# Two long attentions: the first maximum's scores through three rotating bank pairs, with the value projections between them

## The reference: a four-layer perceiver, of which two cross-attentions matter

```python
def _L1_xattn_ref(x, context, Wq, bq, Wk, bk, Wv, bv, Wo, bo):
    q = x @ Wq.T + bq                       # (1, 64, 128), 16 heads of 8
    k = context @ Wk.T + bk                 # (1, 6272, 128)
    v = context @ Wv.T + bv
    ...
    attn = jnp.einsum('bihd,bjhd->bhij', q, k) * SCALE
    attn = jax.nn.softmax(attn, axis=-1)
    out = jnp.einsum('bhij,bjhd->bihd', attn, v)
    out = out.reshape(B, NQ, IN_DIM)
    return out @ Wo.T + bo

x = x + _L1_xattn_ref(_layernorm(x, axis=-1), ctx_768, L1_xattn_Wq, ...)
```

## Time and profile before

| | us |
|---|---|
| median of 3 executions | 663.24 (662.68 to 671.8) |
| the profiled execution | 663.12 |
| its span in the trace | 661.3 |
| level 1: first to last PE instruction of the first maximum | 161.6 to 177.7 |
| level 3: the same | 527.5 to 543.8 |

### The profile page before, as it was taken

The page is one execution under the profiler, slowest core; times in us unless marked ns, Lnnn a source line. Parts: engine busy times, 40 slices in busy tenths (PEclk is TensorE's granted clock), DMA queues, the critical chain, the costliest instruction groups (busy, mean ns, idle before and its releaser), DMA issues. The chain is left out here.

```text
span 661.3 us, 11985 instructions
## 1 busy us (share of the span) xinstructions
PE 513.6 (78%) x4815; PEld 324.5 (49%) x4815; DVE 434.1 (66%) x828; ACT 299.6 (45%) x367; POOL 132.1 (20%) x197
## 2 busy tenths in 40 slices
PE   8799996788889997438995594782578488999857
PEld 5456673575355564313442263472456335556546
DVE  6744325856967955744999999925556596785243
ACT  2578881425557685111654560020112164768611
POOL 2111000000000000204688999400100000000000
PEclk9989997989899999556998587795569679999959
DMA  8364481563200000001022035052300150000000
GB/s 218 72 185 117 128 321 57 173 181 80 94 2 2 1 3 1 3 0 50 0 84 111 0 147 124 5 116 55 127 1 1 31 256 1 2 2 2 2 0 3
DMA packets 17674, 45.59 MB, mean 69 GB/s; under 512 B 4281, under 2 KB 13674, under 8 KB 16778
## 3 DMA queue, kind: packets, MB, share of 16 engines
q1 hardware_dynamic: 17556, 44.72, 22.3%
q0 software_dynamic: 64, 0.11, 0.1%
HBM read 34.28 MB, written 8.29 MB: 64 GB/s over the span
## 5 line engine op out<-in xcount | busy, mean ns | idle before, releaser
L251 POOL TENSOR_TENSOR rstd<-rstd,minus_half 64x1 f32<-64x1 f32 x20 | 11.8, 589 | 420.3 <-DVE rstd L259 420.3
L1497 ACT ACTIVATE ring<-psum,l3x_gain_columns 128x1024 f32<-128x1024 f32 x49 | 54.4, 1114 | 23.2 <-PE psum L1389 23.2
L1497 ACT ACTIVATE ring<-psum,l1x_gain_columns 128x1024 f32<-128x1024 f32 x49 | 54.4, 1114 | 22.4 <-PE psum L1389 22.4
L1403 PE MATMUL psum<-ring,values 128*32 128x128 f32 x1568 | 62.7, 279 | 0.4 <-ACT ring L1497 0.4
L934 ACT ACTIVATE ring<-psum,l0x_key_scale 128x1024 f32<-128x1024 f32 x49 | 52.1, 1114 | 8.2 <-PE psum L827 8.2
L1403 PEld LDWEIGHTS psum<-ring,values 128*32 128x32 f32 x1568 | 37.0, 109 | 28.1 <-issue 24.7
L1602 DVE TENSOR_REDUCE l1x_tops<-psum 128x1 f32<-128x448 f32 x64 | 36.7, 619 | 10.2 <-PE psum L1378 10.1
L1602 DVE TENSOR_REDUCE l3x_tops<-psum 128x1 f32<-128x448 f32 x64 | 36.7, 619 | 10.2 <-PE psum L1378 10.1
L3186 DVE MAX8 l2x_best<-values 128x8 f32<-128x6272 f32 x6 | 40.1, 6691 | 0.1
L3194 DVE MATCH_REPLACE8 values<-l2x_best,values 128x6272 f32<-128x6272 f32 x6 | 40.1, 6675 | 0.0
L827 PE MATMUL psum<-l0x_Q_stack,wide 96*128 96x256 f16 x196 | 29.8, 281 | 4.2 <-ACT ring L934 2.1
(11 more groups left out here) (778 smaller groups left out, 1080.7 us busy)
## 6 DMA issues: line engine op xcount, KB each, us to landing
wide<-keys_aside SPq DMA_DIRECT2D x54, 224.0 KB, 3.8
experts<-in_experts SPq DMA_DIRECT2D x1, 4608.0 KB, 13.5
experts<-in_experts SPq DMA_DIRECT2D x1, 4096.0 KB, 15.3
keys_aside<-ring SPq DMA_DIRECT2D x7, 448.0 KB, 2.5
keys_aside<-experts SPq DMA_DIRECT2D x6, 448.0 KB, 3.2
ring<-in_ctx_tiles SPq DMA_DIRECT2D x1, 2352.0 KB, 9.3
experts<-in_experts SPq DMA_DIRECT2D x1, 2048.0 KB, 7.8
ctx_t<-in_ctx_t SPq DMA_DIRECT2D x3, 672.0 KB, 7.4
```

Source lines behind the costliest of these rows:

```text
L1403: last = nc.tensor.matmul(ps[32 * quarter:32 * quarter + 32, O_BANK, 128 * half:128 * half + 128], mem.values[:, at:at + 32], probs[:, t % ...
L1497: nc.scalar.activation(probs[:, t % PROBS, :].rearrange("p (b n) -> p b n", b=2), ps[:, pair:pair + 2, :], ACT.Exp, scale=exp_gain[:, :]). ...
```

## The change: bank pairs in turn, values in between, queries' stack in halves

The 24 pairs of the first maximum now take the banks (0,1), (2,3), (4,5) in turn, and each pair waits for the reader of the pair three places before it. The values' projections no longer stand ahead of all scores: they use banks 6 and 7, and super `late_values[n]` is projected behind the last pair of round n. It waits until the super before it is copied, and ACT copies super n - 1 behind its two copies of round n. `Q_stack` is announced in two halves of two groups each (`Q_stack0`, `Q_stack1`). DVE copies the stack before the last low parts of the keys, not behind them, and copies the later chunks' stacks and computes the residual behind `raise_top(0)`. Of the two copies that end `raise_top(0)` the second goes to ACT (`first_top`).

```diff
@@ PE
-                    if n >= ready + 2:
-                        pe.wait_ge(values_copied, n - ready - 1)
+                    if n > ready:
+                        pe.wait_ge(values_copied, n - ready)
...
-                        last = nc.tensor.matmul(ps[:, 4 + 2 * (n % 2) + j // 4, (j % 4) * C:(j % 4 + 1) * C],
+                        last = nc.tensor.matmul(ps[:, VALUE_BANKS[j // 4], (j % 4) * C:(j % 4 + 1) * C],
...
-                for n in late_values:
-                    project("V", n)
-                pe.wait_ge(*act_done.at("Q_stack"))
-                pe.wait_ge(*dve_done.at("Q_stack"))
                 if late_keys:
                     pe.wait_ge(low_ready, len(late_keys))
-                pe.wait_ge(values_copied, len(late_values))
-
-                for n, s in first:
+                for n, s, p in pairs:
...
                     pe.wait_ge(*stacked_with(u))
-                    for g in range(G):
-                        if n >= 1 and g % 2 == 0:
-                            pe.wait_ge(*first_read(n - 1, s, g // 2))
-                        last = nc.tensor.matmul(ps[:, s * G + g, 0:HALF], ...
+                    pe.wait_ge(*act_done.at(f"Q_stack{p}"))
+                    pe.wait_ge(*dve_done.at(f"Q_stack{p}"))
+                    if at >= 3:
+                        pe.wait_ge(*first_read(*pairs[at - 3]))
+                    for g in (2 * p, 2 * p + 1):
+                        last = nc.tensor.matmul(ps[:, pair_bank(n, s, p) + g % 2, 0:HALF], ...
+                    last.then_inc(first_scores, 1)
+                    if (s, p) == (1, 1) and n < len(late_values):
+                        project("V", late_values[n])
@@ ACT
-                for n in late_values[0:2]:
-                    copy_values(n)
                 act.wait_ge(*dve_done.at("Q_parts"))
                 for g in range(G):
                     ins = nc.scalar.activation(Q_stack[64:96, 0, g, :], Q_low[32 * g:32 * g + 32, :], ACT.Identity)
-                ins.then_inc(*act_done.mark("Q_stack"))
-                for n in late_values[2:]:
-                    copy_values(n)
+                    if g % 2 == 1:
+                        ins.then_inc(*act_done.mark(f"Q_stack{g // 2}"))
                 for n, s in copied:
...
+                    if 1 <= n <= len(late_values):
+                        copy_values(late_values[n - 1])
+                act.wait_ge(top_turned, 2)
+                nc.scalar.activation(Q_stack[96:98, 0, :, :].rearrange("p g n -> p (g n)")[:, 512:1024],
+                                     ps[96:98, SLOTS[1], :], ACT.Identity).then_inc(*act_done.mark("first_top"))
@@ DVE
-                for n in late_keys[2:]:
-                    low(n)
                 for g in range(G):
                     for block_row in range(2):
                         ins = v.tensor_copy(Q_stack[32 * block_row:32 * block_row + 32, 0, g, :], ...
-                ins.then_inc(*dve_done.mark("Q_stack"))
...
+                    if g % 2 == 1:
+                        ins.then_inc(*dve_done.mark(f"Q_stack{g // 2}"))
+                for n in late_keys[2:]:
+                    low(n)
```

More of the change, by code:

```diff
@@ L1195, in stage_long_attention @@
     late_values = list(range(ready, SUPERS))
-    act_done.stage("Q_stack", *["factors"][:N_CHUNKS - 1])
+    act_done.stage("Q_stack0", "Q_stack1", "first_top", *["factors"][:N_CHUNKS - 1])
     pe_done.stage("xnT", "QT", "own", "projected")
-    dve_done.stage("var", "xn", "xnT", "Q_parts", "Q_stack",
+    dve_done.stage("var", "xn", "xnT", "Q_parts", "Q_stack0", "Q_stack1",
                    *["below", "factor_rows"][:2 * (N_CHUNKS - 1)], "weighed", "OT", "x")
@@ L1217, in stage_long_attention, with queries_with @@
         sem("scores_ready"), sem("probs_ready"), sem("pv_done"), sem("o_saved"))
+    def queries_with(k):
+        return q_ready, 2 * k + 1
     def stacked_with(u):
@@ L1223, in stacked_with, with pair_bank @@
         return stacked, 16 * PER_STACK
+    pairs = [(n, s, p) for n, s in first for p in range(2)]
+    def pair_bank(n, s, p):
+        return 2 * (pairs.index((n, s, p)) % 3)
     def first_read(n, s, p):
@@ L1333, in _ @@
                     project("K", n)
-                for n in late_values:
-                    project("V", n)
-                pe.wait_ge(*act_done.at("Q_stack"))
-                pe.wait_ge(*dve_done.at("Q_stack"))
                 if late_keys:
                     pe.wait_ge(low_ready, len(late_keys))
-                pe.wait_ge(values_copied, len(late_values))
-                for n, s in first:
-                    u, half = n // 2, slice((n % 2) * HALF, (n % 2 + 1) * HALF)
+                for n, s, p in pairs:
+                    u, half, at = n // 2, slice((n % 2) * HALF, (n % 2 + 1) * HALF), pairs.index((n, s, p))
                     pe.wait_ge(*stacked_with(u))
-                    for g in range(G):
-                        if n >= 1 and g % 2 == 0:
-                            pe.wait_ge(*first_read(n - 1, s, g // 2))
-                        last = nc.tensor.matmul(ps[:, s * G + g, 0:HALF], Q_stack[0:96, 0, g, 128 * s:128 * s + 128],
+                    pe.wait_ge(*act_done.at(f"Q_stack{p}"))
[3 more added lines that the diff above has]
+                    for g in (2 * p, 2 * p + 1):
+                        last = nc.tensor.matmul(ps[:, pair_bank(n, s, p) + g % 2, 0:HALF],
+                                                Q_stack[0:96, 0, g, 128 * s:128 * s + 128],
                                                 stack[0:96, u, g, half], start=True, stop=True)
-                        if g % 2 == 1:
-                            last.then_inc(first_scores, 1)
+                    last.then_inc(first_scores, 1)
+                    if (s, p) == (1, 1) and n < len(late_values):
+                        project("V", late_values[n])
                 def turn_top(k):
@@ L1356, in turn_top @@
                     for b in range(2):
-                        bank = slot((q_ready, 2 * k + b + 1))
+                        read = act_done.at("first_top") if k == 0 and b == 1 else (q_ready, 2 * k + b + (k == 0))
+                        bank = slot(read)
                         for j in range(4):
@@ L1384, in scores @@
                     pe.wait_ge(*stacked_with(u))
-                    pe.wait_ge(q_ready, 2 * k + 2)
+                    pe.wait_ge(*queries_with(k))
+                    if t == 0:
+                        pe.wait_ge(*act_done.at("first_top"))
                     if t >= RING:
@@ L1413, in keep_on @@
                                          start=True, stop=True)
-                pe.wait_ge(*first_read(first[-1][0], 0, 0))
+                pe.wait_ge(*first_read(*[pair for pair in pairs if pair_bank(*pair) == 0][-1]))
                 keep_on(14)
@@ L1531, in _ @@
                 v.tensor_tensor(Q_low[:, :], whole, Q_high[:, :], ALU.subtract).then_inc(*dve_done.mark("Q_parts"))
-                for n in late_keys[2:]:
-                    low(n)
+                dve.wait_ge(*dve_done.at("Q_parts"))
                 for g in range(G):
@@ L1558, in raise_top @@
                     for b in range(2):
+                        bank = SLOTS[next(slots) % len(SLOTS)]
+                        if (k, b) == (0, 1):
+                            continue
                         dve.wait_ge(top_turned, 2 * k + b + 1)
-                        bank = SLOTS[next(slots) % len(SLOTS)]
                         v.tensor_copy(Q_stack[96:98, k, :, :].rearrange("p g n -> p (g n)")[:, 512 * b:512 * b + 512],
@@ L1594, in _ @@
                 raise_top(0)
+                dve.wait_ge(*act_done.at("Q_stack1"))
+                dve.wait_ge(*dve_done.at("Q_stack1"))
+                for k in range(1, N_CHUNKS):
+                    v.tensor_copy(Q_stack[0:96, k, :, :], Q_stack[0:96, 0, :, :])
+                step(v.tensor_tensor(residual[:, :], mem.x[:, :], mem.row(f"{pack}_bo"), ALU.add))
                 for k in range(1, N_CHUNKS):
```

18 lines of the change are left out of this document (10 added, 8 removed).

## The result

The changed kernel took 690.06 us (median of 4: 692.68, 690.4, 689.71, 682.83) against 664.88 us before (4: 662.68 to 671.8). The ratio of the means is 1.0343 with a 95% interval of 1.0231 to 1.0454. The direction was right; the median lies 6 us above the range.

The account below looks back on a forecast made before the run. It took the values to bound level 1's start, ACT level 3's, and VectorE's reductions and folds the rounds behind. Terms 0.4 + 14.0 + 0.3 + 0.1 + 0.55 = 15.35 us on 663.12 gave 678.5 us, range 669 to 684.

Parts of the forecast that it names:

- the largest term: Level 1, rounds 1 to 3: PE's new wait for ACT's values copy, two rounds low and one high, +14.0 us.
- the early start that gains nothing: Level 1's start: scores begin 3.85 us earlier, but round 1's first reduction does not come earlier, +0.4 us.
- the lost pair of banks in level 3: Level 3, round 1 to round 2: three pairs deep, 2.88 us where two reductions took 2.0, +0.9 us.
- the end of level 1 with its table behind the small copy: Level 1, end of `raise_top`: ACT's copy ends earlier, but the table load now follows it, +0.1 us.
- Edits at nothing: Last `keep_on`, SP's late keys, layer 3's expert load and the wait before `turn_top`: all claimed to cost nothing.
- "low level throughout" rival: Low clock throughout and the dearer end of each bound: +20.3 us, 683.5 us; chance 0.12.
- The rule of the Trainium skill that the prediction held against the change: Level 1's waits: brief, frequent PE idling makes the clock swing; low rounds dominate by it, 672 us without it.

Follow-up runs that it names:

- f2: e1 without the 29 `keep_on` matmuls that keep PE at work during the folds; ratio 1.0169 to the kernel before.
- e1: Changed kernel, but ACT copies the super of values of round n-1 before its two copies of round n; ratio 1.0187 to the kernel before.
- g1: Changed kernel with four extra matmuls behind the first maximum's transposes and seven behind the first two tiles' scores; ratio 1.0274 to the kernel before.
- the second series: The changed kernel run again with no edit, for a second trace; 689.02 us, ratio 1.0315 to the kernel before.
- e3: Changed kernel with eight extra scores matmuls on PE in front of each super that waits for a copy; ratio 1.0179 to the kernel before.

## Why the prediction was wrong

**Right:** the place and the mechanism of the largest term. PE in front of the supers waits for a copy that ACT makes last, and everything behind it waits too. Worked out +14.0 us, measured +12.6, since a high round was 5.84 and not 6.12, and the low ones 7.73 and 8.22, partly high. With the copy moved, 10.5 us of it went. Also right, each within 0.4 us: the early start that gains nothing, the lost pair of banks in level 3, the end of level 1 with its table behind the small copy. The first of these was partly luck: the scores started 9.4 us into the stage and not 8.35, because the last key projections ran low, and from there to T0 of round 1 it took 6.3 us and not 7.05. In level 1 the table load ended at 204.01 and the exponential started at 204.02. The Trainium skill ("ScalarE: Activation LUTs", "What ACT_TABLE_LOAD costs") has a drain of 1.38 us beside the 1.28 of the load; this trace shows none, and the measurement decides.

**The step that failed** is "Edits at nothing": "The last `keep_on` waits for one later reader, hidden in the folds." I put it at nothing without working out how long it lasts at either level. At the high level the 29 matmuls took 5.66 us, and the transposes followed 0.6 us behind `turn` (200.86 and 201.47, level 1); mostly at the low one they took 8.43 and stood in front of the transposes (level 3): +2.6 us against the first trace of before and +1.9 against the second, whose own keep-on ran partly low. That they are the queue is shown by f2: 3.5 us from folds to cast without them, where e1 with them has 7.0 and 6.7. And no term at all stood for the clock at the head of the main loop: +3.5 and +3.3 us. That it is the clock is shown by g1; what brings the fall is open. These three are 9.4 us; 15.35 with them and with the smaller rounds is 23.3, as much as the two stages together grew, and the ratio of the second series, 1.0315, is 21 us. The "low level throughout" rival priced the low level only inside the changed rounds (its sum is 683.4, not 683.5), so the range ended at 684. That the rest of the profiled difference, 6.3 us, fell outside the change was not foreseen either; before's own executions lie in two groups, about 664 and 672 us, which the three shown had hinted at.

The rule of the Trainium skill that the prediction held against the change ("TensorE: Matmul & The Clock Gate", "A second HAM failure mode: psum-queue depth-cycling") pointed the right way: with PE idle at each of these waits the level swung, and filling the idle pieces took 4.3 us away (e3).

## What to carry to other kernels

When a change opens gaps on TensorE, price the low level not only where the gaps are but for every piece of TensorE work behind them whose length the schedule took for granted, fillers above all. Matmuls put in to keep the clock are a queue in front of the real work once the clock is low (8.43 us here, where 5.66 were nearly hidden). And before putting work "in between", write down for each wait in it which engine satisfies it and what stands ahead of that on its list.

## What the runs showed that I had not expected

- A table load on ScalarE behind its last copy costs 1.28 us and then nothing: the exponential followed 0.01 us later.
- Eleven useless matmuls in front of a loop shortened each loop by 3.0 to 3.5 us (g1 against the changed kernel).
- One unchanged program took mostly about 664 or about 672 us, and one unchanged stretch 11.8 or 14.4 us from variant to variant. A change of 5 us cannot be told in a single execution here; the traces show it stage by stage, with the low level's own wandering of 1 to 2 us a stage.
